# Residual rows written into the output early, and the last scatter made to add to them

## The reference

```
x = x + s * g                                  # end of layer 0; x is the residual of layer 1
xn = layernorm(x)
s = mamba(xn)                                  # a state space scan over 1024 steps
# mixture of 8 experts, 2 rounds; expert chosen per token
w, idx = top_k(softmax(xn @ gate_W + gate_b), 2)
e0 = expert[idx0](xn);  e1 = expert[idx1](xn + 0.5 * e0)
g = silu(layernorm(xn + w0 * e0 + w1 * e1) * gamma + beta)
x = x + s * g                                  # the output
```

## Time and profile before

| | |
|---|---|
| median of three runs | 2205.34 us (2202.84 to 2207.92) |
| the profiled execution | 2196.74 us |
| its span, from the first to the last instruction | 2195.0 us |
| busy share of the span | PE 85%, DVE 76%, ACT 58%, POOL 55% |
| second expert round | about 2008 to 2195 us |

### The profile page before, as it was taken

The page is one execution under the profiler, slowest core; times in us unless marked ns, Lnnn a source line. Parts: engine busy times, 40 slices in busy tenths (PEclk is TensorE's granted clock), DMA queues, the critical chain, the costliest instruction groups (busy, mean ns, idle before and its releaser), DMA issues. The chain is left out here.

```text
span 2195.0 us, 26582 instructions
## 1 busy us (share of the span) xinstructions
PE 1872.7 (85%) x8596; PEld 1061.4 (48%) x8596; DVE 1670.2 (76%) x2189; ACT 1264.9 (58%) x1685; POOL 1217.7 (55%) x651
## 2 busy tenths in 40 slices
PE   5689988998998898789879898999885677998996
PEld 3345545654654463233334332533242235887885
DVE  4874797497579525899999999999989995232787
ACT  4864874576477414666655665466544334665774
POOL 2701810350180002688888999989976674222576
PEclk9999999999999999999999999999999989999998
DMA  7420641443054106898899899988899984223453
GB/s 202 98 57 15 140 101 53 115 96 98 23 131 97 77 24 52 279 316 292 272 314 315 264 275 301 305 296 284 285 300 363 328 322 148 99 97 100 139 160 105
DMA packets 177321, 402.68 MB, mean 183 GB/s; under 512 B 48174, under 2 KB 77104, under 8 KB 176034
## 3 DMA queue, kind: packets, MB, share of 16 engines
q1 hardware_dynamic: 165154, 371.09, 54.7%
q0 software_dynamic: 12032, 29.90, 4.7%
HBM read 356.30 MB, written 45.51 MB: 183 GB/s over the span
## 5 line engine op out<-in xcount | busy, mean ns | idle before, releaser
L1336 POOL TENSOR_TENSOR late<-late,rows 128x1024 f32<-128x1024 f32 x256 | 603.3, 2365 | 147.9 <-DVE late L1816 141.4
L1987 PE MATMUL m_Q<-late,ident_m 128*128 128x512 f32 x1024 | 529.4, 649 | 152.7 <-POOL late L1336 115.0
L1816 DVE TENSOR_TENSOR_SCAN late<-m_Q,late 128x1024 f32<-128x1024 f32 x256 | 586.3, 2290 | 45.1 <-ACT m_Q L1522 17.0
L1522 ACT ACTIVATE m_Q<-late,acol 128x1024 f32<-128x1024 f32 x256 | 286.0, 1117 | 363.2 <-DVE late L1816 361.7
L1987 PEld LDWEIGHTS m_Q<-late,ident_m 128*128 128x128 f32 x1024 | 195.9, 203 | 452.4 <-POOL late L1336 251.3
L1809 DVE TENSOR_TENSOR late<-m_Q,rows 128x1024 f32<-128x1024 f32 x256 | 307.0, 1199 | 13.3 <-DMA rows<-bc_s 13.2
L553 DVE SCALAR_TENSOR_TENSOR early<-early,work 128x1024 f32<-128x1024 f32 x128 | 155.9, 1218 | 44.8 <-ACT early L699 42.9
L2050 PE MATMUL m_Q<-late 128*128 128x128 f32 x1248 | 158.9, 281 | 8.9 <-issue 1.3
L2050 PEld LDWEIGHTS m_Q<-late 128*128 128x128 f32 x1248 | 147.1, 194 | 36.3 <-issue 35.0
L709 ACT ACTIVATE early<-early 128x1024 f32<-128x1024 f32 x128 | 135.2, 1056 | 29.9 <-DVE early L558 29.0
L710 ACT ACTIVATE early<-early,halfpi 128x1024 f32<-128x1024 f32 x128 | 145.8, 1139 | 0.0
(11 more groups left out here) (243 smaller groups left out, 3344.3 us busy)
## 6 DMA issues: line engine op xcount, KB each, us to landing
rows<-bc_s SPq DMA_DIRECT2D x512, 512.0 KB, 5.8
rows<-st_s SPq DMA_DIRECT2D x64, 384.0 KB, 5.8
r_s<-late SPq DMA_DIRECT2D x39, 256.0 KB, 2.0
rows<-st_s SPq DMA_DIRECT2D x64, 128.0 KB, 6.4
st_s<-early SPq DMA_DIRECT2D x8, 768.0 KB, 5.4
xin<-in_x SPq DMA_DIRECT2D x4, 1024.0 KB, 5.7
xres<-in_x SPq DMA_DIRECT2D x4, 1024.0 KB, 5.6
mx_s<-s SPq DMA_DIRECT2D x4, 1024.0 KB, 4.5
```

The source lines that it names most:

```text
L1336: nc.gpsimd.tensor_tensor(pr[:, n % NH, :], h[:, n % NH, :], cb[:, n % NCB, :], ALU.mult).then_inc(pr_ok, 1)
L1522: A(dA[:, :], dt[:, (b * KI + m) % 2, :], ACT.Exp, scale=acol[:, m, i % NS:i % NS + 1]).then_inc(dA_ok, 1)
L1816: v_.tensor_tensor_scan(h[:, n % NH, :], dA[:, :], dB[:, n % 2, :], 0.0, ALU.mult, ALU.add).then_inc(h_ok, 1)
L1987: ins = mm(half(Y, c), ident[:, :], half(pr[:, n % NH, :], c), start=False, stop=(n % NS == NS - 1), skip_group_check=True)
```

## The change

`sums_out` stores the residual straight into the output tensor, in layer 0. `mx_s` shrinks to the 256 columns of `s`. `finish` on DVE only multiplies. The scatter `finished` gets `compute_op=ALU.add`: the DMA adds its rows to what stands in the output. The semaphore `fin` counts one for each tile in place of two.

```diff
                 def sums_out(b):
                     sp.wait_ge(x1_ok, b + 1)
-                    sp.dma_start(tokens(g["mx_s"][bass.ds(b * L, L), D:2 * D]), s1[:, :, :]).then_inc(stored, 16)
+                    sp.dma_start(tokens(g["out"][b]), s1[:, :, :]).then_inc(stored, 16)
...
-        mx = part(rows, NF * D, [NX, 2 * D])
+        mx = part(rows, NF * D, [NX, D])
...
-                    sp.dma_start(g["mx_s"][b * L:(b + 1) * L, 0:D].rearrange("(t p) d -> p t d", p=P), so[:, :, :]).then_inc(stored, 16)
+                    sp.dma_start(g["mx_s"][b * L:(b + 1) * L, :].rearrange("(t p) d -> p t d", p=P), so[:, :, :]).then_inc(stored, 16)
...
                 def last_rows(n):
                     if n >= NX:
-                        pool.wait_ge(fin, 2 * (n - NX) + 2)
+                        pool.wait_ge(fin, n - NX + 1)
                     nc.gpsimd.indirect_dma_start(mx[:, n % NX, :], None, g["mx_s"], index(1, n, 1)).then_inc(mx_in[n % NX], 16)
 
                 def finished(n):
-                    pool.wait_ge(fin, 2 * n + 2)
-                    nc.gpsimd.indirect_dma_start(g["out"].rearrange("b n d -> (b n) d"), index(1, n, 2), f[:, n % NF, :], None, bounds_check=B * L - 1, oob_is_err=False).then_inc(og_out[n % NF], 16)
+                    pool.wait_ge(fin, n + 1)
+                    nc.gpsimd.indirect_dma_start(g["out"].rearrange("b n d -> (b n) d"), index(1, n, 2), f[:, n % NF, :], None, bounds_check=B * L - 1, oob_is_err=False, compute_op=ALU.add).then_inc(og_out[n % NF], 16)
...
-                    v_.tensor_tensor(dst, dst, mx[:, n % NX, 0:D], ALU.mult).then_inc(fin, 1)
-                    dv.wait_ge(fin, 2 * n + 1)
-                    v_.tensor_tensor(dst, dst, mx[:, n % NX, D:], ALU.add).then_inc(fin, 1)
+                    v_.tensor_tensor(dst, dst, mx[:, n % NX, :], ALU.mult).then_inc(fin, 1)
```

More of the change, by code:

```diff
@@ L2102, in blocks @@
 def blocks(nc, g):
-    for name, shape, dt in (("xn1_s", [B, L, D], F32), ("xn1T_s", [B, P, KD, L], F32), ("mx_s", [B * L, 2 * D], F32), ("bc_s", [B, 2 * NS, L], F32),
+    for name, shape, dt in (("xn1_s", [B, L, D], F32), ("xn1T_s", [B, P, KD, L], F32), ("mx_s", [B * L, D], F32), ("bc_s", [B, 2 * NS, L], F32),
                             ("ext0_s", [NTILE * P, 4], I32), ("ext1_s", [NTILE * P, 4], I32), ("r1_s", [NTILE * P, 2 * D], F32), ("st_s", [4, 8, DH, 3, L], BF16)):
```

## The result

The changed kernel is slower: ratio 1.0048 of its time to that of before, 95% interval 1.0033 to 1.0063. On the 2202.5 us median of before that is +10.6 us (+7.3 to +13.9); forecast were +8.4.

What follows compares the result with a forecast made beforehand. PE was taken to set the steady pace and a POOL chain the end; POOL would become the bound. +7.6 us for the adding scatters and +0.8 landing made +8.4 on 2205.3, so 2213.7 us, 8 in 10 within 2202.5 to 2228.

Steps and rivals of the forecast that it cites:

- What bounds the kernel, and POOL's room: Second expert round: PE sets the steady pace, POOL fills 3.90 of 4.07 us per tile, and a POOL chain sets the end.
- Stores and gathers: 0 us: Layer 0 and scan stores to other addresses, and half-size gathers of `mx_s`, would change the time by 0 us.
- DVE's line 1904: -0.9 us: Without this instruction in `finish` on DVE, `finish(30)` ends earlier and the last twelve DMAs start 0.9 us sooner.
- The price x = 0.47 us: Each adding scatter costs POOL 0.47 us more, half a gather, between 0 and 1.03; 37x - 9.8 gives +7.6 us.
- Landing: +0.8 us: An adding scatter lands 0.8 us later, the difference between a DRAM gather's 3.6 and a scatter's 2.8 us.
- What is late next: PE's rows for tile 38 come 7 us later, still 12 us early; the buffers `f` also suffice, so delay stays on POOL.
- POOL's room covering it: Rival: x at most 0.32, so POOL's waits absorb the price; +1.3 us, up to +2.8, no change told; chance 0.33.
- The gain that stays: Rival: the addition leaves DVE and x stays below 0.1; -0.9 us, at most -1.8; chance 0.10.
- the DMA engines: Rival: adding packets over 2.4 times as long make the DMA engines the bound; +70 us at four times; chance 0.05.

Runs made afterwards that it cites:

- e1_plain_scatter: The changed kernel with the plain scatter put back, residual addition left out: ratio 1.0002 to before; 179.4 us from first gather to last scatter's start, against 193.1 changed.
- e6_before_join8: The kernel before with JOIN 8 in place of 11, gathers of mx_s issued three tiles sooner: 180.7 us from first gather to last scatter's start, as before.
- e2_add_only: The kernel before with only its scatter made adding, DVE still adding the residual: ratio 1.0083; 194.9 us from first gather to last scatter's start, against 180.7.
- e5_scatter_shapes: The changed kernel with scatters varied by tile, adding or plain, 128, 64 or 32 rows: adding minus plain 0.60, 0.55 and 0.49 us of POOL.
- e8_after_join8: The changed kernel with JOIN 8 in place of 11, gathers of mx_s three tiles sooner: 189.1 us from first gather to last scatter's start, against 193.1.

## Why the prediction was right

*What bounds the kernel, and POOL's room.* Right, and it is what the forecast stood on. The count of instructions and gaps (3.90 of 4.07 us) foretold that 0.3 us more would fill POOL. The runs with nineteen early and late adding scatters show the waits taking up what comes early.

*Stores and gathers: 0 us.* Not contradicted. `e1_plain_scatter` has all of them and is 1.3 us faster in the stretch, but the stores lie ahead of it. For them there is only the time of the whole: the ratio's upper end, 1.0022, leaves them some 6 us at most. The first gather starts at 2008.7, 2010.5 and 2015.9 us with the stores of before (before, `e6_before_join8`, `e2_add_only`) and at 2002.1 to 2013.2 in the eight profiles with the new ones, so none of it shows. The half rows changed the median landing of the gather of `mx_s` from 3.6 to 3.0 us, and its POOL time hardly (0.971 and 0.996 us). That the count of rows matters for POOL's time was nearly wrong: a plain scatter of 32 rows still takes 0.90 us of the 1.02 of 128.

*DVE's line 1904: -0.9 us.* Right within what one profile tells: -1.3 us with plain scatters, and lost in the changed kernel, where POOL no longer waits.

*The price x = 0.47 us.* Mis-sized: it is 0.61. With it, 37 x 0.61 - 9.8 is +12.8 us; measured are +13.0 to the end of the last scatter. The formula was right, as far as one profile of each kernel tells, and this term was short by 0.14 us, 5.2 us in the sum. The reason given for x (half of a gather, as one more list of addresses) was wrong though the size was near: three quarters of the price don't depend on the rows (`e5_scatter_shapes`). That argument would have misled for a scatter of few rows.

*Landing: +0.8 us.* Wrong. An adding scatter does land later while other DMAs are under way: the median rose from 2.8 to 3.8 us, 0.4 more than the price, and from 2.5 with plain scatters and half rows (`e1_plain_scatter`). But the last ones come when the others are done (the queue holds 20.2% of the engines in the last 14.5 us). From the start of the last scatter to the end of the span it is 5.65 us before and 6.33 after, 0.68 more, and 0.57 of that is POOL's own longer time, which the term of x already held. The row "to landing" counts from the issue; its minimum rose from 2.1 to 2.7, by the price. So I counted part twice, and at the end of the program 0.1 us was right.

*What is late next.* PE's rows for tile 38 were issued 10 us later on the count from the first gather (2156.03 - 2011.09 against 2143.68 - 2008.69), where 7 were forecast with x = 0.47; PE didn't wait for them, as said. That 10 would follow with 0.61 is in part chance: I had counted 21 scatters where there are 20 (9.3 us), and the other rows of POOL are 0.5 us longer there. Not foreseen: `finish` on DVE waits for its gather, 13.6 us in all, because I had looked at the leads of lines 1421 and 1430 and taken that of line 1426 for granted. `e8_after_join8` took 11.4 us of these waits away, with a gain that the moved gathers explain by themselves.

*The rivals.* POOL's room covering it needed x under 0.32. The gain that stays needed x under 0.1; the two kernels with plain scatters show its size, 1.3 us with JOIN 11 and 3.5 with JOIN 8. For the DMA engines I took 8 packets of each for a plain scatter, 1.4 us. The first nine gathers alone move 720 packets, 80 each; two such gathers for each of 39 tiles leave 1872 of the 8112, so a plain scatter has 48 packets, 3 for each engine, and the adding one 144, 9 for each. The added 0.67 us of each engine stay under the 1.9 that I had found free.

*How near it came.* The traces put the change at 13.0 us to the end of the last scatter and 0.1 behind it, 4.7 us over the forecast's 8.4. The ratio gives +10.6, with 7.3 to 13.9, and holds both. So the nearness of 8.4 to 10.6 is partly luck, and that of 2213.7 to the median of 2212.4 us more so: I had started from 2205.3, where 20 executions of the kernel before have 2202.5.

GPSIMD Engine Reference of the Trainium skill (section 4, When to use GPSIMD) has such a DMA described by two cores, one for reads and one for writes. A price above 0 agrees with that. But read as two loads for one core it would let the whole price grow with the rows, 0.60 us over 128 or 4.7 ns for each; measured are 1.2 ns beside a fixed 0.45 us.

## What to carry to other kernels

An engine that issues DMAs is fuller than its busy share says: count its instructions in one round of the loop, add the gap that stands between them even when nothing is waited for, and compare with the loop's period. Before moving work from an engine that is covered to one that is nearly full, write the sum as price times count minus the waits that can take it up, and see which of the count stands behind the last wait. When an engine has become full in one stretch, look for instructions that may be issued ahead of that stretch, where it still waits. And to read what a DMA costs the DMA engines, compare kernels that move the same bytes: a share of the engines that stays the same can hide a price.

## What the runs showed of the hardware

An indirect DMA of GpSimd that adds takes 1.62 us of POOL at 128 rows, 1.49 at 64 and 1.39 at 32, against 1.02, 0.94 and 0.90 for a plain one, whether the rows have 512 bytes or 1 KB. I had expected a price by rows. The engines that move the data pay too: 144 packets in place of 48 for the same bytes, and 0.67 us more of each of the 16. It lands later by 1.0 us in the median (2.8 to 3.8), of which 0.6 are POOL's own; the last one of the program ends it by 0.7 us later after its start, of which 0.6 are POOL's.
